# A two-layer decoder kernel: in the first stage, value product and output blocks are issued in turns

## The reference

```
x = x + tanh(g_xattn[0]) * L0_attention(layernorm(x), ctx)    # stage 1: the stage that is changed
x = x + tanh(g_ffn[0])   * L0_ffn(layernorm(x))               # stage 2: mixture of low-rank adapters
x = x + tanh(g_xattn[1]) * L1_attention(layernorm(x), ctx)    # stage 3: causal attention
x = x + tanh(g_ffn[1])   * L1_ffn(layernorm(x))               # stage 4
```

```
q_r, k_r = query and rotated context, projected to 64 per head
attn     = softmax(q_r @ k_r.T)            # 128 x 128 per head and sequence
ctx_c    = attn @ kv_rope                  # the value product, 128 wide
out      = sum over heads of ctx_c @ G_h   # G_h = w_kc_kv and Wo multiplied together, 128 x 512
```

## Time and profile before

| | before |
|---|---|
| median of three runs | 1342.37 us |
| lowest, highest | 1339.96, 1342.41 us |
| span of the profiled execution | 1340.5 us |
| TensorE busy in it | 1318.1 us (98%) |
| VectorE, ScalarE, GpSimd busy | 937.1, 518.3, 403.5 us |
| stage 1, by the first and the last output product | about 58 to 440 us |

### The profile page before, as it was taken

How to read it: one execution, slowest core, us unless ns; L and a number is a source line. 1 busy time by engine, 2 the same in 40 slices (tenths; PEclk the granted TensorE clock), 3 DMA queues, 4 the chain that set the end, 5 groups by cost and what they waited for, 6 DMA issues and landing times.

```text
span 1340.5 us, 20295 instructions
## 1 busy us (share of the span) xinstructions
PE 1318.1 (98%) x7372; PEld 1066.2 (80%) x7372; DVE 937.1 (70%) x1813; ACT 518.3 (39%) x1569; POOL 403.5 (30%) x461
## 2 busy tenths in 40 slices
PE   7999999999999999999999999999998899999998
PEld 6788888888887788778887888788886677778877
DVE  5766676675775878785678667776888788846643
ACT  3545455454564331231123111321126777832220
POOL 4212323231256243101120112113525866630000
PEclk9999999999999999999999999999999999999999
DMA  8755454443572232210221112112324556555651
GB/s 299 229 166 163 144 174 138 156 155 127 183 221 86 84 87 71 83 40 16 58 77 49 34 40 87 44 48 67 94 87 146 194 182 200 165 197 176 215 168 55
DMA packets 137415, 167.70 MB, mean 125 GB/s; under 512 B 16076, under 2 KB 89932, under 8 KB 137316
## 3 DMA queue, kind: packets, MB, share of 16 engines
q1 hardware_dynamic: 137316, 166.42, 39.2%
HBM read 111.83 MB, written 54.53 MB: 124 GB/s over the span
## 4 chain that ended last, share of the span: by engine, by line
PE 91%; DVE 4%; ACT 2%; DMA 2%; issue 0%; POOL 0%; SPq 0%; DVEq 0%; ACTq 0%; POOLq 0%
PE bank L118 89%; PE bank L121 2%; ACT P L124 1%; DVE sm L146 0%; DVE AH L130 0%; DVE st L152 0%; DVE STG L130 0%; SPq L170 0%; DMA pscr<-STG 0%; DMA PTV<-pscr 0%; DMA STG<-in_WqT_dram 0%; DMA XR<-in_x_dram 0%; ACT bank L124 0%; DMA XR<-in_ctx_dram 0%; DVE AH L127 0%
## 5 line engine op out<-in xcount | busy, mean ns | idle before, releaser
L118 PE MATMUL bank<-XT,AR 128*128 128x512 f32 x1152 | 280.1, 393 | 0.1
L118 PE MATMUL bank<-AR 128*128 128x512 f32 x1056 | 257.6, 395 | 0.0
L118 PEld LDWEIGHTS bank<-XT,AR 128*128 128x128 f32 x1152 | 213.9, 188 | 48.3 <-issue 1.5
L124 ACT ACTIVATE STG<-bank,b1c 128x512 f32<-128x512 f32 x128 | 88.4, 690 | 387.4 <-PE bank L118 313.6
L118 PEld LDWEIGHTS bank<-AR 128*128 128x128 f32 x1056 | 194.5, 188 | 47.8 <-issue 3.7
L118 PE MATMUL bank<-AR,CT 128*128 128x512 f32 x768 | 191.3, 392 | 0.0
L118 PE MATMUL bank<-AR,AH 128*128 128x512 f32 x768 | 185.8, 390 | 0.0
L127 DVE CAST AH<-STG 128x512 fp32r<-128x512 f32 x192 | 90.3, 470 | 113.2 <-PE bank L118 99.3
L118 PEld LDWEIGHTS bank<-AR,AH 128*128 128x128 f32 x768 | 143.6, 188 | 30.7 <-issue 1.1
L118 PEld LDWEIGHTS bank<-AR,CT 128*128 128x128 f32 x768 | 140.1, 188 | 27.0 <-issue 0.4
L127 POOL CAST BA<-STG 128x256 fp32r<-128x256 f32 x64 | 30.6, 478 | 396.5 <-PE bank L118 252.0
(11 more groups left out here) (144 smaller groups left out, 1816.2 us busy)
## 6 DMA issues: line engine op xcount, KB each, us to landing
XR<-scr SPq DMA_DIRECT2D x64, 256.0 KB, 3.0
pscr<-PYZ SPq DMA_DIRECT2D x30, 512.0 KB, 2.9
PYZ<-pscr SPq DMA_DIRECT2D x120, 128.0 KB, 3.0
XR<-in_x_dram SPq DMA_DIRECT2D x32, 256.0 KB, 3.8
XR<-lscr SPq DMA_DIRECT2D x128, 64.0 KB, 2.0
scr<-XR SPq DMA_DIRECT2D x32, 256.0 KB, 2.1
pscr<-STG SPq DMA_DIRECT2D x16, 512.0 KB, 2.6
PTV<-pscr SPq DMA_DIRECT2D x64, 128.0 KB, 2.8
```

Of the source, the lines that this page charges most:

```text
L118: return self.e.matmul(o, w, x, start=start, stop=stop, skip_group_check=True) if self.e else Nothing()
L124: return self.e.activation(o, x, func, **kw) if self.e else Nothing()
```

## The change

In 15 of the 32 steps, value product and output blocks 2 and 3 are no longer separate groups of six. A new function `wo_pv1(u, b, half)` issues one long product of output block b of unit u, then one short product of value half `half` of unit u+1, and so on, 12 instructions per call. It waits first for everything that both need: the value result of unit u, the free bank, and PT of unit u+1 (`pz_ok[u + 1]`).

Output block 1 of the unit before is held back: it is issued at the end of step u no more but in step u+1 between k and the two mixed groups. `late(u)` names the steps after which a block is held back: u from 8 to 30 with u % 8 in 0, 1, 4, 5, 6. The mixed groups are then in step u+1, that is in steps 9, 10, 13, 14, 15, 17, 18, 21, 22, 23, 25, 26, 29, 30 and 31. The number of products of each kind and their operands are the same. The lists of the other engines are the same.

```diff
+            def mm1(part, o, w, x, start, stop):
+                return pe.matmul(o, w[part == 0], x[part == 1], start and part == 0, stop and part == 2)
...
+            def wo_pv1(u, b, half):
...
+                if p == 0:
+                    ps.take(("acc", m, b), b)
+                    pe.wait_ge(*ps.free(("acc", m, b)))
+                pe.wait_ge(*ps.drained(("pv", u, b // 2)))
+                pe.wait_ge(*ps.drained(("G", p, 1)))
+                pe.wait_ge(*ps.free(key))
+                pe.wait_ge(*pz_ok[u + 1])
+                pe.wait_ge(*kvl_ok[(u + 1) // 8])
+                for j in range(2):
...
+                    for part in range(3):
+                        ins = mm1(part, ps.banks[b][:, :], (CT[:, s], CT[:, s2]), GG[p][j], p == 0 and j == 0,
+                                  p == 7 and j == 1)
+                        pv = mm1(part, k[:, 256 * j:256 * j + 256].rearrange("p (j t) -> p j t", j=2), (hi[:, t], lo[:, t]),
+                                 (v[:, 0, :, t], v[:, 1, :, t]), True, True)
...
+            def late(u):
+                return 8 <= u < NU - 1 and u % 8 in (0, 1, 4, 5, 6)
...
-                if 4 <= u < NU:
-                    wo1(u - 4, (2,))
-                if 3 <= u < NU:
-                    pv1(u - 3, (0,))
-                if 4 <= u < NU:
-                    wo1(u - 4, (3,))
...
-                if 3 <= u < NU:
-                    pv1(u - 3, (1,))
+                if late(u - 1):
+                    wo1(u - 4, (1,))
+                    wo_pv1(u - 4, 2, 0)
+                    wo_pv1(u - 4, 3, 1)
+                else:
...
                 if 3 <= u < NU:
-                    wo1(u - 3, (0, 1))
+                    wo1(u - 3, (0,) if late(u) else (0, 1))
```

More of the change, by code:

```diff
@@ L711, in wo1 @@
                         ins.then_inc(*wo_ok.mark((u, half)))
+            def wo_pv1(u, b, half):
+                m, p = divmod(u, 8)
+                key = "pv", u + 1, half
+                k = ps.take(key, ring4.next())
+                hi, lo = halves(KVL, 512)
+                v = PT[:, :].rearrange("p (h j t) -> p h j t", h=2, j=2)
+                if p == 0:
[7 more added lines that the diff above has]
+                for j in range(2):
+                    n = 2 * b + j
+                    s, s2 = slice(128 * n, 128 * n + 128), slice(1024 + 128 * n, 1152 + 128 * n)
+                    t = slice(128 * (2 * half + j), 128 * (2 * half + j) + 128)
+                    for part in range(3):
[3 more added lines that the diff above has]
+                                 (v[:, 0, :, t], v[:, 1, :, t]), True, True)
+                if p == 7:
+                    ins.then_inc(*ps.fill(("acc", m, b)))
+                elif b % 2:
+                    ins.then_inc(*wo_ok.mark((u, b // 2)))
+                pv.then_inc(*ps.fill(key))
+            def late(u):
+                return 8 <= u < NU - 1 and u % 8 in (0, 1, 4, 5, 6)
             def router_mm(m, bank):
@@ L845, in tensor @@
                     k1(u)
-                if 4 <= u < NU:
-                    wo1(u - 4, (2,))
-                if 3 <= u < NU:
-                    pv1(u - 3, (0,))
-                if 4 <= u < NU:
-                    wo1(u - 4, (3,))
-                if u + 1 < 8:
-                    prep_b(u + 1)
-                if 3 <= u < NU:
-                    pv1(u - 3, (1,))
+                if late(u - 1):
[3 more added lines that the diff above has]
+                else:
+                    if 4 <= u < NU:
+                        wo1(u - 4, (2,))
+                    if 3 <= u < NU:
+                        pv1(u - 3, (0,))
+                    if 4 <= u < NU:
+                        wo1(u - 4, (3,))
+                    if u + 1 < 8:
+                        prep_b(u + 1)
+                    if 3 <= u < NU:
+                        pv1(u - 3, (1,))
                 if u < NU and p == 7 and m + 1 < NM:
```

## The result

Nine runs of the changed kernel have a median of 1344.58 us (1343.60 to 1345.54), nine of the kernel before on the same chip 1341.43 us. The ratio is 1.0023, 95% interval 1.0015 to 1.0032: about 3.1 us slower. The profiled execution took 1345.28 us, with a span of 1343.5 against 1340.5.

What follows compares the result with a forecast made beforehand. TensorE's product spacing was taken to bound the kernel. The turns' 1.4 us less and the stalls' 2.6 more gave 1342.4 + 1.2 = 1343.6 us, range 1340.2 to 1346.2 (the forecast's own range 1342.0 to 1345.2).

Steps and rivals of the forecast that it cites:

- What bounds it: Steps 8 to 30: TensorE busy 270.50 of 270.50 us at clock 1.00, so the stage lasts as its products are spaced.
- Part 1, the turns: Mixed steps: twelve long-short pairs take 4.10 us instead of 4.20, 1.4 us less in all.
- The residual of a switch: In the turns, each switch from short to long leaves a tenth or two of its 0.02 us.
- The sign that I had named: A mixed step's 24 products take about 4.1 us from the first to the start of output block 0.
- Part 2, the held-back block: Six long products, 1.36 us, move from before the scores to behind k; nothing is added.
- Part 3, the wait for PT: Output block 2's first product waits for PT 1.36 us earlier; steps 29 and 30 stall 1.3 each, 2.6 us more.
- My longer way from PT to the product: Step 29, taking the earlier trace's delay from PT to product: start at 373.73, 1.37 us late.
- the shorter way: Step 29, judged by step 3's PT-to-product delay and a block 0.07 longer: 1.30 us late.
- The thin steps 13, 14, 21 and 22: Steps where VectorE works without a pause; 0.21 us to spare before PT is wanted, so no cost.
- Rival 1: Steps 29 and 30: no stall, as VectorE's sign change comes first or GpSimd's splits start later; 1341.0 us; chance 0.22.
- Rival 2: Mixed steps: each switch from short to long costs its full 0.02 us, 3.0 more, with stalls 1348.0; chance 0.15.
- Rival 3: Steps 13, 14, 21, 22, and 15 or 23 stall too, 0.1 to 0.2 us each, 1344.4 in all; chance 0.08.

Runs made afterwards that it cites:

- The two experiments that remove the collision: Changed kernel with GpSimd's weight splits of steps 28 to 30 moved later: 1353.85 us; changed kernel with VectorE's row maximum negated by its reduce: 1343.38 us.
- the same version: Changed kernel with GpSimd's weight splits of steps 28 to 30 put behind its next division of attention weights: 1353.85 us against 1342.85, ratio 1.0087.

## Why the prediction was right or wrong

- **What bounds it.** Right. Stage 1 was the sum of TensorE's spacings, and all of the loss arises there: 0.5 us in twelve mixed steps without a wait, and 2.7 in steps 29 to 31, which is nearly all the two waits.
- **Part 1, the turns.** Wrong in sign. The step that failed is "the short one costs half a long one (0.113), since its weight load now lies beside a long product". I read the 0.007 between 0.113 and 0.120 as a loss that better company would cure. The long product beside it did not cure it: in the cheap pattern a pair costs 0.347, which is 0.227 + 0.120. With weights of 128 columns every product of 256 to 512 columns pays the same 13 ns beyond its columns; two widths more would have told the two readings apart, and the earlier trace rows fit both. That the weight load has no part in it is not shown: with 64-column weights the pair fell to 0.340. The residual of a switch was mis-sized as well: I gave it a tenth or two of 0.02, and it was 0.007, a third. The sign that I had named, about 4.1 us for a mixed group, did not come; it was 4.23. Forecast 1.4 us less in all, measured 0.52 more in twelve steps, some 0.6 in fifteen; my bounds (0.333 to 0.366 a pair) held 0.353.
- **Part 2, the held-back block.** Right: 0.0 forecast and measured.
- **Part 3, the wait for PT.** Right in place, in number and in cause. Forecast 1.3 a step, measured 1.36 and 1.38 (less 0.07 in step 30 from cheaper pairs). My longer way from PT to the product gave 1.37, but that it fits is chance: it had 0.24 us from PT's end to the product, and the changed kernel shows 0.15 and 0.14. The rest is the first long product, 0.08 longer than usual, as the shorter way had it (0.10 + 0.07). The 0.24 of the earlier trace rows was the schedule of a product that did not wait. The thin steps 13, 14, 21 and 22 did not wait.
- **The sum.** 1.2 us forecast, 3.1 measured; the gap of 1.9 is nearly all part 1 (1.4 less against some 0.6 more). The range 1340.2 to 1346.2 held 1344.58, also as a difference (2.2 less to 3.8 more). The narrower range of the forecast itself, up to 1345.2, held the time only by luck: as a difference it ends at 2.8, and the kernel before measured 0.9 lower than in the three runs that I started from. The sign was right because the stall was; in part 1 it was wrong. The chances were less good: no change had 0.70, and 0.23% lies just beyond its bound of 0.2%, where I had put 0.24.
- **Rivals.** Rival 1 did not occur: GpSimd's split started 0.03 to 0.05 us ahead of the sign change in steps 29 and 30 of each version that keeps both instructions in their old places. That both hang on the same `ve<-mv` would explain it. The two experiments that remove the collision show that the stall goes with it. Rival 2 had the right direction for the turns and a third of its price. Its condition came true, a short product at 0.120 and more than 0.004 a switch: the turns gained nothing, and the stalls stood alone. Rival 3 did not occur.

The rule of the Trainium skill on the shared port (SBUF — State Buffer, section Who interferes with whom) agrees with these runs: 1.27 us for the sign change behind the split, 0.17 without it, and a reduce from PSUM untouched beside it.

## What to carry to other kernels

Before products are mixed to hide something, show that there is something to hide: run one size by itself at three or four widths, and see whether the spacing is columns plus a constant; run it with smaller weights too, which was left out here. When two groups with different waits are merged, the merged group waits for the later of them at its first instruction; list the slack of every instance, not the typical one, since here 13 of 15 had room and two did not. And where an engine is late by a collision, shorten its own list before reordering the other's: what is queued behind the moved work, DMA issues among them, is moved too.

## What the runs showed of the hardware that I had not expected

- A product with 128 rows and 128 weight columns costs (columns + 32)/2.4 ns at 256, 320, 384 and 512 columns, and 112 ns at 192 and at 128.
- Alternating 512 and 256 columns settles into one of two patterns with weights of 128 columns, 0.347 or 0.353 us a pair, by the product ahead; banks and the operand's shape made no difference (4.231 us each time). With 64 weight columns it is 0.340.
- Behind 2.8 us of idle time ahead of a product (4.3 us from the start of the last six) the granted clock was 0.50 for about 3 us. Behind the next idle time, 2.3 us in step 31 of the same version, it fell to 0.51 as well, 1.2 us after TensorE had started again. Behind the 1.1 us waits of the changed kernel it stayed at 1.00. What one wait costs is then not its length alone: the twelve turns behind the first took 5.71 us instead of 4.23.
